# Summing attention weights in layer 0: the two halves of the keys folded into one before TensorE sums them

## What is computed

```python
qh = (q @ Wq + bq).reshape(Bn, Tq, H, DK)          # H = 16, DK = 64
kh = (k @ Wk + bk).reshape(Bn, Tk, H, DK)          # Tk = 128 keys
vh = (v @ Wv + bv).reshape(Bn, Tk, H, DK)
attn = jnp.einsum('bqhd,bkhd->hbqk', qh, kh) * mask[None]
attn = attn - jnp.max(attn)
attn = jnp.exp(attn) * mask[None]
attn = attn / (jnp.sum(attn, axis=-1, keepdims=True) + 1e-15)
out = jnp.einsum('hbqk,bkhd->bqhd', attn, vh).reshape(Bn, Tq, H * DK)
out = out @ Wo + bo                                 # then residual and layer norm
```

## Time and profile before

| | us |
|---|---|
| median of 3 runs | 835.83 |
| lowest, highest | 835.52, 836.83 |
| the profiled execution | 838.48 |
| its span on the core | 836.5 |

### The profile page before, as it was taken

The page is one execution under the profiler, slowest core; times in us unless marked ns, Lnnn a source line. Parts: engine busy times, 40 slices in busy tenths (PEclk is TensorE's granted clock), DMA queues, the critical chain, the costliest instruction groups (busy, mean ns, idle before and its releaser), DMA issues.

```text
span 836.5 us, 12619 instructions
## 1 busy us (share of the span) xinstructions
PE 818.0 (98%) x4564; PEld 553.5 (66%) x4564; DVE 554.9 (66%) x1278; ACT 454.9 (54%) x575; POOL 478.5 (57%) x311
## 2 busy tenths in 40 slices
PE   8999999999999999998999999999999999999996
PEld 6777475756666575475668677587686775876744
DVE  3568676667676676866764855756648557567577
ACT  4415363736455554726474673864755738647262
POOL 2022404031231403355889989899889898996636
PEclk9999999999999999999999999999999999999999
DMA  9508534251617053799192461562623714612002
GB/s 305 216 24 299 192 131 179 89 217 51 232 42 259 18 203 103 237 334 248 46 220 67 136 193 39 142 174 73 197 72 126 202 38 139 176 51 76 1 26 76
DMA packets 73661, 118.13 MB, mean 141 GB/s; under 512 B 27776, under 2 KB 34176, under 8 KB 73600
## 3 DMA queue, kind: packets, MB, share of 16 engines
q1 hardware_dynamic: 72640, 117.00, 44.6%
q10 hardware_dynamic: 960, 0.34, 0.2%
HBM read 77.47 MB, written 34.08 MB: 133 GB/s over the span
## 4 chain that ended last, share of the span: by engine, by line
PE 83%; DMA 5%; DVE 3%; SPq 3%; issue 2%; POOL 2%; ACT 2%; DVEq 0%; POOLq 0%; ACTq 0%
PE bank L545 19%; PE bank L547 18%; PE bank L546 18%; PE bank L607 6%; PE bank L577 6%; PE bank L584 6%; PE bank L747 3%; PE bank L766 3%; DMA wk_sb<-wk 1%; DMA sums_dram<-sums_out 1%; DVE scores L1397 1%; DMA r_dram<-den 1%; DMA u_dram<-u_out 1%; PE bank L533 1%; DMA r_bc<-r_dram 1%
## 5 line engine op out<-in xcount | busy, mean ns | idle before, releaser
L1639 POOL TENSOR_TENSOR x_lo<-x_raw,x_hi 128x2048 fp32r<-128x2048 f32 (+1 forms) x8 | 35.6, 4450 | 196.5 <-ACT x_hi L930 180.8
L545 PE MATMUL bank<-wo_lo,a_hi 128*128 128x512 f32 x320 | 127.7, 399 | 1.5 <-DVE z L1371 1.5
L546 PE MATMUL bank<-wo_hi,a_lo 128*128 128x512 f32 x320 | 124.7, 390 | 0.0
L547 PE MATMUL bank<-wo_hi,a_hi 128*128 128x512 f32 x320 | 124.7, 390 | 0.0
L1248 DVE CUSTOM_DVE_ANT_0 scores<-bank,mask_f 128x512 f32<-128x512 f32 x128 | 80.9, 687 | 51.9 <-PE bank L577 51.9
L1681 POOL TENSOR_TENSOR a_lo<-a_raw,a_hi 128x1024 fp32r<-128x1024 f32 x32 | 78.0, 2438 | 45.3 <-ACT a_hi L1025 44.5
L545 PE MATMUL bank<-x_lo,wq_hi 128*128 128x512 f32 x256 | 101.2, 395 | 0.6 <-DVE q_lo L1237 0.6
L546 PE MATMUL bank<-x_hi,wq_lo 128*128 128x512 f32 x256 | 99.8, 390 | 0.0
L547 PE MATMUL bank<-x_hi,wq_hi 128*128 128x512 f32 x256 | 99.7, 390 | 0.0
L942 ACT ACTIVATE q_hi<-bank,bq_sb 128x512 fp32r<-128x512 f32 x64 | 44.1, 690 | 101.1 <-PE bank L547 97.9
L1070 ACT ACTIVATE scores<-scores,sh 128x512 f32<-128x512 f32 x128 | 80.2, 711 | 25.1 <-DVE sh L1422 25.0
(11 more groups left out here) (183 smaller groups left out, 1732.7 us busy)
## 6 DMA issues: line engine op xcount, KB each, us to landing
u_dram<-u_out SPq DMA_DIRECT2D x8, 2048.0 KB, 7.6
a_raw<-u_dram SPq DMA_DIRECT2D x32, 512.0 KB, 4.2
r_bc<-r_dram SPq DMA_DIRECT2D x56, 256.0 KB, 5.0
x_raw<-x_t SPq DMA_DIRECT2D x8, 1024.0 KB, 5.6
xn<-x_n SPq DMA_DIRECT2D x8, 1024.0 KB, 5.3
xb_dram<-xn SPq DMA_DIRECT2D x8, 1024.0 KB, 6.0
z<-xb_dram SPq DMA_DIRECT2D x32, 256.0 KB, 2.8
out<-z SPq DMA_DIRECT2D x6, 1024.0 KB, 4.8
```

The source lines that it names most:

```text
L545: nc.tensor.matmul(dst, lh, rl, start=first, stop=False)
L546: nc.tensor.matmul(dst, ll, rh, start=False, stop=False)
L547: return nc.tensor.matmul(dst, lh, rh, start=False, stop=last)
```

## The change

For blocks 0 to 6 the sums are made in another way. Once the probabilities of a group of four heads are masked, a DMA from SP's queue (`copy_halves`) copies 64 of their 128 partitions to the other 64 partitions of a new tile `folds` (for groups 0 and 2 the upper half of the keys goes to the lower partitions, for 1 and 3 the lower to the upper), and the half that stayed is added to the copy: group 0 by VectorE (`fold_first`), groups 1, 2 and 3 by GpSimd (`fold`). `folds` then holds two heads on the partitions, and `sums_folded(i)`, eight matmuls in two steps in place of sixteen in four, stands behind all logits of the next block. Block 7 keeps the old sums.

With that go these moves: the next block's `mask_scores` waits for the fold of the group whose scores it writes over; GpSimd's order becomes fold 1, fold 2, half of `x_low`, fold 3, the other half, `x_and_bias`; `queries0` waits for the two halves of `x_low` separately; ScalarE saves two of the value products before `x_high` instead of after it; `query_bias` moves between the `q_low` of block 1, and GpSimd doesn't wait for it any more; `x_and_bias(7)` stands ahead of the folds of block 6 and waits for no mask product; `copy_halves(i)` stands in SP's queue behind `store_xb(i)` and ahead of `load_xn(i + 1)` (block 0: ahead of `store_xb(0)`, block 6: behind `load_xn(7)`); `g1_b` is loaded later, ahead of `store_sums(7)`, since `folds` shares its place; the steps of the maxima count on one semaphore instead of five.

```diff
+            def copy_halves(i):
+                if i > 0:
+                    sp.wait_ge(sums_psum_ready, i)
+                for j in range(HG):
+                    sp.wait_ge(probs_ready, HG * i + j + 1)
+                    sp.dma_start(fold_of(j), copied_half(j)).then_inc(half_copied[j], 16)
...
+            def sums_folded(i):
+                pe.wait_ge(first_folded, i + 1)
+                pe.wait_ge(folded, (HG - 1) * (i + 1))
+                if i > 0:
+                    pe.wait_ge(u_saved, (C0 + 1) * i)
+                for step in range(2):
+                    for g in range(G):
+                        last = nc.tensor.matmul(SUM_BANK[32 * g:32 * g + 32, :], summer[:, HG + step, :],
+                                                folds[:, G * step + g, :], start=(step == 0), stop=(step == 1))
+                last.then_inc(sums_psum_ready, 1)
...
-                if j == 0 and i > 0:
-                    pe.wait_ge(u_saved, (C0 + 1) * i)
-                last = row_sums(SUM_BANK, j)
-                if j == HG - 1:
-                    last.then_inc(sums_psum_ready, 1)
+                if i == NB - 1:
...
                     for c in range(2 * j, 2 * j + 2):
                         logits0(i, c)
+                sums_folded(i - 1)
                 if i + 1 < NB:
                     queries0(i + 1)
...
                     mask_float(i)
+                    save_u(i - 1, 0, 2)
                     x_high(i + 1)
-                    save_u(i - 1)
+                    save_u(i - 1, 2)
...
+                    if i > 0 and h % HG == 0:
+                        if h == 0:
+                            dve.wait_ge(first_folded, i)
+                        else:
+                            dve.wait_ge(folded, (HG - 1) * (i - 1) + h // HG)
...
+            def fold_first(i):
+                dve.wait_ge(half_copied[0], 16 * (i + 1))
+                nc.vector.tensor_tensor(fold_of(0), fold_of(0), kept_half(0), ALU.add).then_inc(first_folded, 1)
...
-                if i == 0:
-                    for c in range(C1):
-                        query_bias(c)
+                    if i == 0:
+                        for part in BIAS_AFTER.get(c, ()):
+                            query_bias(part)
+                fold_first(i)
...
+            def fold(i, j):
+                if j == 1:
+                    pool.wait_ge(xb_ready, i + 1 if i + 2 < NB else NB)
+                elif j == 3 and i + 2 < NB:
+                    pool.wait_ge(x_ready, low_count(i + 2) - 1)
+                pool.wait_ge(half_copied[j], 16 * (i + 1))
+                nc.gpsimd.tensor_tensor(fold_of(j), fold_of(j), kept_half(j), ALU.add).then_inc(folded, 1)
...
+            for i in range(NB - 1):
+                if i == NB - 2:
+                    x_and_bias(i + 1)
+                fold(i, 1)
+                fold(i, 2)
+                if i + 2 < NB:
+                    x_low(i + 2, 0)
+                fold(i, 3)
+                if i + 2 < NB:
+                    x_low(i + 2, 1)
+                    x_and_bias(i + 1)
```

More of the change, by code:

```diff
@@ L247, in cross_attention_program @@
             "q_psum_ready q_hi_ready q_ready logits_ready masked_ready")
-        tile_max_ready, row_ready, quad_ready, top_ready, run_max_ready, shift_ready = sems(
-            "tile_max_ready row_ready quad_ready top_ready run_max_ready shift_ready")
+        max_step_ready, shift_ready = sems("max_step_ready shift_ready")
+        MAX_STEPS = 11
         exp_ready, probs_ready, u_psum_ready, sums_psum_ready, u_saved = sems(
             "exp_ready probs_ready u_psum_ready sums_psum_ready u_saved")
+        half_copied = [sem(f"half_copied{j}") for j in range(HG)]
+        first_folded, folded = sems("first_folded folded")
         m_eps_ready, mhalf_ready, eps_ready, den_ready, rec_ready = sems(
@@ L372, in _ @@
             sp.dma_start(ident[:], identity).then_inc(ident_loaded, 16)
-            for dst, src in ((bo0_b, bo0), (g0_b, gamma0), (bb1_b, bo1), (g1_b, gamma1)):
+            for dst, src in ((bo0_b, bo0), (g0_b, gamma0), (bb1_b, bo1)):
                 sp.dma_start(dst[:], src.partition_broadcast(P)).then_inc(consts_loaded, 16)
@@ L402, in _ @@
                     store_xb(i)
-                    load_xn(i + 1)
+                    if i + 2 < NB:
+                        copy_halves(i)
+                        load_xn(i + 1)
+                    else:
+                        load_xn(i + 1)
+                        copy_halves(i)
             def load_u(i, n):
@@ L478, in _ @@
             sp.dma_start(s_stage[:, 2048:4096].rearrange("p (c n) -> p c n", c=C1), chunks(wo1)).then_inc(w1_loaded, 16)
+            sp.dma_start(g1_b[:], gamma1.partition_broadcast(P)).then_inc(be1_loaded, 16)
             store_sums(NB - 1)
@@ L563, in queries0 @@
                         cols = slice(c * P, (c + 1) * P)
+                        if c == 0 and k == KC // 2:
+                            pe.wait_ge(x_ready, low_count(i))
                         last = split_product(A_BANKS[c % 2][:], (wq0_hi[:, k, cols], wq0_lo[:, k, cols]),
@@ L1635, in _, with x_low @@
         def _(pool):
-            def x_low(i, chunks=KC):
+            def x_low(i, half):
                 pool.wait_ge(x_hi_ready, i + 1)
-                ks = slice(0, chunks)
+                if i >= 2:
+                    pool.wait_ge(folded, (HG - 1) * (i - 2) + 2 + half)
+                ks = slice(half * KC // 2, (half + 1) * KC // 2)
                 nc.gpsimd.tensor_tensor(x_lo[:, ks, :], x_raw[:, ks, :], f(x_hi[:, ks, :]),
@@ L1652, in _ @@
             nc.gpsimd.tensor_tensor(ctx_lo[:], ctx_sb[:], f(ctx_hi[:]), ALU.subtract).then_inc(ctx_ready, 1)
-            x_low(0, KC // 2)
-            for i in range(NB):
-                if i == 1:
-                    pool.wait_ge(bq1_ready, C1)
-                if i + 1 < NB:
-                    x_low(i + 1)
-                if i == 0:
-                    pool.wait_ge(consts_loaded, 16 * 6)
-                    nc.gpsimd.tensor_tensor(bb1_b[:], bb1_b[:], beta0_b, ALU.add).then_inc(bb1_ready, 1)
-                x_and_bias(i)
+            x_low(0, 0)
+            x_low(1, 0)
+            x_low(1, 1)
+            pool.wait_ge(consts_loaded, 16 * 5)
+            nc.gpsimd.tensor_tensor(bb1_b[:], bb1_b[:], beta0_b, ALU.add).then_inc(bb1_ready, 1)
+            x_and_bias(0)
+            for i in range(NB - 1):
[6 more added lines that the diff above has]
+                fold(i, 3)
+                if i + 2 < NB:
+                    x_low(i + 2, 1)
+                    x_and_bias(i + 1)
+            pool.wait_ge(folded, (HG - 1) * (NB - 1))
             for half in range(2):
@@ L1758, in out_scale @@
             def out_scale(i, half):
+                if i == 0 and half == 0:
+                    pool.wait_ge(be1_loaded, 32)
                 pool.wait_ge(n1_ready, QT * i + 2 * half + 2)
@@ L1773, in out_bias @@
             def out_bias(i, half):
-                if i == 0 and half == 0:
-                    pool.wait_ge(be1_loaded, 16)
                 pool.wait_ge(ng1_ready, 2 * i + half + 1)
```

88 lines of the change are left out of this document (54 added, 34 removed).

## The result

The changed kernel takes 864.29 us (median of 4 runs, 863.62 to 866.4), the kernel before 835.67 on the same chip (834.55 to 836.83): 1.0347 times as long, 95% interval 1.0324 to 1.0369. The profiled execution after has a span of 864.6 us against 836.5, so 28.1 us are to be found in the trace.

What follows compares the result with a forecast made beforehand. It took PE to bound the kernel (busy 818.0 of 836.5 us). Terms 9 + 8.8 + 4.0 - 0.9 + 1 = +21.9 us gave span 858.4, median 857.7; range 824 to 866.

Steps and rivals of the forecast that it cites:

- PE's gain: Blocks 0 to 6: sums removed save 3.5 us, eight added matmuls cost 1.93; net -1.54 a block, -10.8 for seven.
- The prices of the parts: Per block: VectorE add 2.28 us, GpSimd add 4.6 (bounds 2.35 and 4.6), copy 4.2 (bounds 2.8 and 6.0).
- The port: SBUF access: a two-SBUF-input VectorE operation and a GpSimd operation exclude each other; each waits for the whole of the other.
- Rival 1: Port doesn't matter for adds on half the partitions, or PE never meets them: 827 us; chance 0.26.
- rival 4: GpSimd keeps the port from add 1 to add 2, VectorE's add waits 4.6 us more: over 875; chance 0.05.
- A middle block: Blocks 1 to 5: late masks and GpSimd's third add make PE wait; 41.0 instead of 39.2 us, +1.8 each.
- T: The start of the values of a block on PE; times in a block are counted from it in us.
- Block 0: Query biases take turns with GpSimd's adds for SBUF, delaying logits and sums: 26.6 instead of 17.8 us, +8.8.
- Blocks 5 and 6: Block 5 like the other middle ones, +1.8; in block 6 x_and_bias(7) delays the fourth mask product, +4.0.
- the landing of the last residual tile: Block 6: x_and_bias(7)'s tile arrives about T-5.0, in the third product, so GpSimd holds up the fourth product.
- the predicted -0.9: Values of block 7: exponentials ready ahead of PE, giving back its 0.9 us of idle.
- The row broadcast in SP's queue: The g1_b load ahead of store_sums(7) in SP's queue: +0 to +1.4 us, taken +1.

Runs made afterwards that it cites:

- The wait moved by experiment: Against the changed kernel, x_and_bias(7) waits for all mask products of block 6, as before the change: 859.51 us, ratio 1.027.
- 831.5: Only groups 2 and 3 folded, both by GpSimd, two waits added, and ScalarE's rounding of the output weights earlier: 831.47 us, ratio 0.9955.
- 827.8: Changed kernel with all four adds cut to one element a partition and the last residual add behind block 6's products: 827.83 us, ratio 0.9903.
- half of the folds: Against the changed kernel, only groups 2 and 3 folded, both by GpSimd, no VectorE add, two waits added: 832.05 us, ratio 0.9946.
- both moved waits: Changed kernel with GpSimd's block 0 adds waiting for the biases and the last residual add for block 6's probabilities: 859.98 us, ratio 1.0283.
- half adds: Changed kernel with GpSimd's three adds over two of the four heads of a group (64 x 1024): 857.45 us, ratio 1.0246.

## Why the prediction was right, and where it was off

It was slower by the predicted mechanism, and 864.29 lies in the range, 6.6 above the 857.7 and 0.3 above the 850 to 864 of its own forecast. By its own steps:

- **PE's gain, -1.54 a block**: 37.66 against 39.19 with tiny adds.
- **The prices of the parts**: GpSimd's add 4.57 us on 64 partitions (taken 4.6, bound 2.35), VectorE's 2.27, the copy 4.2 as taken:

```profile
folds<-scores SPq DMA_DIRECT2D x28, 512.0 KB, 4.2
```

- **The port**: the exclusion also holds between the two halves of the partitions (3.87 beside GpSimd's add, 2.27 with that add tiny). Rival 1, the only way to a faster kernel, falls with that. The measured order, one turn each, also rules out rival 4. The rule of the Trainium skill, page "SBUF — State Buffer", section "Who interferes with whom", agrees in each of these rows, but not in who goes first in block 0 (last section).
- **A middle block, +1.8**: +1.7. VectorE's add ends at T+5.4 (predicted 5.5), masks start at T+5.6 (5.5), add 2 ends at T+9.8 (10.1), add 3 at T+17.0 (17.0), the folded sums start at T+17.1 (17.0).
- **The clock**: the sum has no term for it. PE's busy time is 39.9, 40.0 and 24.5 us in blocks 0, 5 and 6, and 37.7, 37.7 and 23.1 with all adds tiny: after its waits PE runs matmuls at the lower clock, and most of these 5.9 us are that. A part of this is hidden by waits that were shorter than predicted.
- **Block 0, +8.8**: +8.6, but by luck, from two errors that cancel. Logits begin at T+10.4 instead of T+11.7: bias 0 slipped in ahead of add 1, so biases 1 and 2 were the two that waited, and behind add 2 only bias 2 and q_lo 7 were left, without bias 1 and q_lo 6. Then PE, after 8.44 us of waiting, ran at a granted clock of 0.50 for its first 2.9 us and still at 0.65 for the next 2.8, and the folded sums start at T+24.5 (24.6).

```profile
83.38 0.68 DVE L1366 CUSTOM_DVE_ANT_0 w_stage<-w_stage 128x512 f32<-128x512 f32 x1
...
83.99 5.01 DVE L1366 CUSTOM_DVE_ANT_0 w_stage<-w_stage 128x512 f32<-128x512 f32 x1
...
89.59 4.31 DVE L1366 CUSTOM_DVE_ANT_0 w_stage<-w_stage 128x512 f32<-128x512 f32 x1
```

- **Blocks 5 and 6, predicted +1.8 and +4.0, measured +7.0 and +5.8**: this is the term that was mis-sized, by 7.0 us together; the smaller misses take 0.8 of it back in the trace, and the median stands 0.4 us nearer to the span than before. The step that failed is the landing of the last residual tile "at about T-5.0, in the third product". By its own numbers it is T-5.8 (17.1 ahead of T, and 6.0 and 5.3 for the transfers), 0.6 us behind the start of that product. But in this place the store took 4.3 us, not 6.0, and the load 5.8, from 324.58 till GpSimd starts at 330.42:

```profile
320.31 0.38 SPq L348 DMA_DIRECT2D xb_dram<-xn  x1
324.58 0.39 SPq L344 DMA_DIRECT2D xn<-x_n  x1
```

  The tile was there at T-6.7 of the T that a block of 40.9 would give (337.1), 0.3 us ahead of product 3 (330.76). So two products were blocked instead of one. The delayed third one is what block 5 pays for: PE stood 3.39 us in the queries (at 337.88), and its matmuls took 1.9 us more at a granted clock of 0.96, together the 5.3 above 40.9. Two runs show the two cases apart. With VectorE's add tiny the residual add came behind the start of product 3 and held up product 4 alone (6.04 us): block 5 took 39.0, like the blocks before it. With GpSimd's adds tiny it held up product 3 alone, and block 5 took 43.2 against 38.3. The wait moved by experiment brings block 5 to 40.9 and the whole to 859.5, near the forecast.
- **In block 6** the folded sums end at T+21.4, as predicted, again from two errors: VectorE's add ends at T+7.9 instead of T+9.4, and PE then runs matmuls at the lower clock. What is over the +4.0 is a second meeting that wasn't foreseen. The divisor's addition of a constant stands behind GpSimd's split of the output weights, and PE waits 2.16 us ahead of the values of block 7:

```profile
367.11 3.98 DVE L1396 TENSOR_SCALAR den<-den,eps 64x128 f32<-64x128 f32 x1 [0.37 <-ACT eps L1078]
```

```profile
366.47 4.53 POOL L1759 TENSOR_TENSOR wo_lo<-wo_stage,wo_hi 128x2048 fp32r<-128x2048 f32 x1 [2.22 <-ACT wo_hi L1018]
```

The split is late because ScalarE rounds the second half of the weights behind its copy of the sums out of PSUM, and the folded sums of block 6 now come behind all logits of block 7. ScalarE's rows, the copy and the rounding:

```profile
364.00 0.60 ACT L1035 ACTIVATE sums_out<-bank 128x512 f32<-128x512 f32 x1 [2.84 <-PE bank L641]
364.49 1.90 ACT L1018 ACTIVATE wo_hi<-wo_stage 128x2048 fp32r<-128x2048 f32 x1
```

The copy starts at T+21.6, in the kernel before at T+15.7 (335.36). So this is a price of the later sums and not of the adds: with all adds tiny PE waits 2.18 us there. In the kernel before, the addition met only the last 0.5 us of the split and took 0.55; where GpSimd does nothing it takes 0.29. Of PE's idle of 0.9 us in the values of block 7, 0.67 stayed (10.85 busy of 11.52), so of the predicted -0.9 there came -0.3.
- **The row broadcast in SP's queue, +1**: it holds the queue for 2.56 us, and no cost is seen: the program behind layer 0 is 0.3 us shorter. But that part takes 475.7 to 480.2 us in the profiles here, so a term of 1 us is neither shown nor ruled out.

What was not tried: other orders of GpSimd's work in blocks 5 and 6, a residual add after the last products of block 7, and all four folds with the output weights rounded earlier. So it stays open how much of the distance from 831.5 to 827.8, and below, can be had.

## What to carry to other kernels

Before work goes to an idle GpSimd, list the VectorE operations with their operands in SBUF within its reach: in these traces each meeting costs VectorE up to the whole of GpSimd's operation, and the two take turns from there, so place the added work where VectorE reads PSUM (here 9.2 us of adds a block, for which PE never waited) rather than where GpSimd happens to be idle. Where the arrival of a transfer decides which engine asks first, a median of its rows isn't enough: work the block out for both orders. A part of a change can be worth more than the whole: half of the folds, with VectorE's add gone and the two waits moved, gave 0.5% where all of them lost 3.5% (2.8% with the same two waits moved).

## What the runs showed of the hardware that was not expected

- VectorE on partitions 0 to 63 and GpSimd on 64 to 127 exclude each other as on all partitions (3.87 us against 2.27), and an add of one element a partition waits just so (1.74 us).
- A VectorE operation with one input tensor and a scalar in SBUF, 64 x 128, waited as well: 3.98 us beside GpSimd's split, 0.29 where GpSimd does nothing; the masks with one input in PSUM never did (0.69). By the same section of the Trainium skill, a copy or an operation with a scalar can use both ports of VectorE and then excludes GpSimd; the row agrees.
- With both engines waiting, the port went to the one and the other by turns: products of 6.41 and 5.97 us, then an add of 5.33. Strict order of asking it is not: GpSimd's add 1 of block 0 asked at 82.13, and bias 0, at 83.38, still had its 0.68 us. Why is open.
- A short idle of PE can cost more than itself, and its length doesn't tell when. In the changed kernel PE idled 1.69 and 0.25 us between logits, and the granted clock stayed 1.00 over blocks 1 to 4. With both moved waits it idled the same 1.69 and 0.26 in blocks 1 and 2, ran at 0.54 from 181 to 183 us, and these blocks took 41.6 and 41.5 us at 0.96 instead of 40.9. With half adds it idled 1.94 and 0.26, and three of four middle blocks had 0.96 and took 1.1 to 1.5 us more than the one at 1.00.
